# Second attention layer: h in 20 pieces with two own PSUM banks, rectified scores in SBUF

## The reference

```python
h = (x @ W).reshape(N, heads, out_ch)          # N = 1024; x has 1024 values, heads * out_ch = 512
a_src = jnp.einsum('nhc,hc->nh', h, att_src)
a_dst = jnp.einsum('nhc,hc->nh', h, att_dst)
e = jax.nn.leaky_relu(a_src[src] + a_dst[dst], 0.2)
m = jax.ops.segment_max(e, dst, num_segments=N)
ex = jnp.exp(e - m[dst])
s = jax.ops.segment_sum(ex, dst, num_segments=N)
out = jax.ops.segment_sum(h[src] * (ex / (s[dst] + 1e-16))[:, :, None], dst, num_segments=N)
```

## Time and profile before

| | us |
|---|---|
| median of 3 runs | 1220.42 |
| span of the profiled execution | 1220.4 |
| second attention layer, first sum of GpSimd to last `counted` | 906.59 to 1123.65 |
| busy over the span: PE, DVE, ACT, POOL | 1052.0, 778.0, 524.2, 625.3 |

### The profile page before, as it was taken

One profiled execution on the slowest core, in us unless ns is written; L12 is line 12 of the kernel. 1 busy time (PEld: TensorE's weight loads), 2 busy tenths in 40 slices (PEclk: granted clock), 3 DMA queues, 4 the chain that ended last, 5 costly groups with the idle time before them and its releaser, 6 DMA issues. The chain is left out here.

```text
span 1220.4 us, 17917 instructions
## 1 busy us (share of the span) xinstructions
PE 1052.0 (86%) x5617; PEld 744.6 (61%) x5622; DVE 778.0 (64%) x1724; ACT 524.2 (43%) x752; POOL 625.3 (51%) x503
## 2 busy tenths in 40 slices
PE   3999899989599999999298799888898888777897
PEld 1454577778477777777055488787773434433575
DVE  6988578628233333332495889996368777787855
ACT  2234544231111111111133478889537776766323
POOL 1000458302557555543410587999478777685242
PEclk9999899855599999999589799999989999989899
DMA  3000003044388999992510111211012111172551
GB/s 117 1 0 1 1 1 137 2 170 151 132 285 296 301 302 307 303 306 94 182 35 1 37 45 43 87 53 36 9 39 69 36 53 35 37 242 72 179 173 42
DMA packets 107987, 134.57 MB, mean 110 GB/s; under 512 B 30240, under 2 KB 76040, under 8 KB 107792
## 3 DMA queue, kind: packets, MB, share of 16 engines
q1 hardware_dynamic: 92720, 112.68, 28.4%
q0 software_dynamic: 15200, 21.04, 5.3%
HBM read 135.03 MB, written 27.45 MB: 133 GB/s over the span
## 5 line engine op out<-in xcount | busy, mean ns | idle before, releaser
L2347 POOL TENSOR_TENSOR am<-CT,qb 128x1024 f32<-128x1024 f32 x128 | 302.2, 2385 | 29.5 <-ACT PT L2376 17.4
L2369 ACT ACTIVATE PS<-adb,ab 128x1024 f32<-128x1024 f32 x128 | 143.1, 1118 | 89.4 <-DVE am L2474 88.2
L2474 DVE TENSOR_TENSOR am<-PS,am 128x1024 f32<-128x1024 f32 x128 | 156.4, 1222 | 37.3 <-ACT PS L2369 30.2
L2468 DVE CUSTOM_DVE_ANT_0 masked<-PS,mask 128x1024 f32<-128x1024 f32 x128 | 156.2, 1220 | 32.4 <-issue 30.6
L2580 PE MATMUL PS<-PT,h 128*65 128x512 f32 x256 | 122.8, 611 | 36.6 <-ACT PT L2376 25.1
L1232 DVE COPY yo<-PS 128x512 f32<-128x512 f32 x64 | 44.3, 691 | 168.5 <-PE PS L1170 163.1
L2567 PE MATMUL PS<-h,PT 128*128 128x129 f32 x1024 | 128.0, 283 | 22.0 <-ACT PT L2376 12.2
L2376 ACT ACTIVATE PT<-am,as 128x1024 f32<-128x1024 f32 x128 | 145.2, 1134 | 0.3 <-DVE am L2474 0.3
L2567 PEld LDWEIGHTS PS<-h,PT 128*128 128x128 f32 x1024 | 121.1, 196 | 30.5 <-issue 18.2
L1197 ACT ACTIVATE hT<-PS,b1T 128x128 f32<-128x128 f32 x128 | 40.0, 363 | 214.8 <-PE PS L1162 195.7
L1162 PE MATMUL PS<-xgT,w1r 128*128 128x128 f32 x1024 | 125.8, 276 | 0.0
(11 more groups left out here) (426 smaller groups left out, 1777.9 us busy)
## 6 DMA issues: line engine op xcount, KB each, us to landing
w2r<-in_L_ffn_W SPq DMA_DIRECT2D x64, 512.0 KB
w1r<-in_L_ffn_W SPq DMA_DIRECT2D x64, 512.0 KB
adb<-a_scratch SPq DMA_DIRECT2D x16, 512.0 KB, 4.0
qb<-q_scratch SPq DMA_DIRECT2D x14, 512.0 KB, 3.8
wc<-in_L_gnn_W SPq DMA_DIRECT2D x4, 1024.0 KB, 9.2
w1x<-in_L_ffn_W SPq DMA_DIRECT2D x2, 2048.0 KB, 11.0
w2x<-in_L_ffn_W SPq DMA_DIRECT2D x2, 2048.0 KB, 9.3
w1x<-in_L_ffn_W SPq DMA_DIRECT2D x7, 512.0 KB, 5.4
```

Source lines behind the costliest of these rows:

```text
L2347: pool.tensor_tensor(am[:, k % RING, :], CT[:, s, :], qb[:, hd % 2, :], ALU.add).then_inc(s_sum, 1)
L2369: act.activation(RELU, adb[:, hd % 2, :], ACT.Relu, bias=ab[:, s, hd:hd + 1]).then_inc(s_relu, 1)
L2468: dve.tensor_tensor_reduce(masked[:], wide(row_bank(hd)), mask[:, t, :], 1.0, -3.0e38, ALU.subtract, ALU.max, mrow[:, hd % 2, t:t + 1]).th ...
L2474: dve.tensor_tensor(am[:, k % RING, :], RELU, am[:, k % RING, :], ALU.add).then_inc(s_all, 1)
```

## The change

The rectified scores of the second layer go to a new tile `rl` in SBUF instead of banks 4 and 5. These two banks go to the pieces of h that are made between the pairs, in turn. Those pieces are 20 of one tile by 128 columns instead of ten of twice that, behind 20 pairs; a piece waits only for the copy of the piece two before it, and `rows` waits for no piece. Copies come two pairs behind instead of three. The first attention layer stays as it was.

```diff
+        rl = place("rl", [P, N], F32, 102 * KIB)
...
-            RELU = wide(4)
+            RELU = rl[:] if final else wide(4)
...
             def unit_bank(i):
-                return i % 2 if final else (0, 3, 0)[i]
+                if final:
+                    return i % 2 if i < H0 else 4 + i % 2
+                return (0, 3, 0)[i] if i < H0 else 3
...
-                UNITS = [[(t, 0, slice(0, FH), slice(0, FH))] for t in range(NT)] + quarters
-                H0 = 6
-                H_AT = (0, 1), (0, 3), (1, 1), (1, 5), (2, 1), (2, 5), (3, 5), (4, 1), (4, 5), (5, 1)
+                UNITS = [[(t, 0, slice(0, FH), slice(0, FH))] for t in range(UP_FRONT)]
+                for half, tiles in ((0, range(UP_FRONT, NT)), (1, range(NT))):
+                    UNITS += [[(t, half, slice(q * FQ, (q + 1) * FQ), slice(0, FQ))] for q in range(2) for t in tiles]
+                H0 = UP_FRONT
+                FIRST_HALF = UP_FRONT + 2 * (NT - UP_FRONT)
+                H_AT = ((0, 1), (0, 2), (0, 3), (0, 4),
+                        (1, 1), (1, 4), (1, 6), (2, 1), (2, 4), (2, 6), (3, 0), (3, 3),
+                        (3, 5), (3, 7), (4, 1), (4, 4), (4, 6), (5, 1), (5, 4), (5, 6))
...
-            LATE = 3 if final else 2
+            LATE = 2
...
-                            sp.wait_ge(s_h, NT)
+                            sp.wait_ge(s_h, FIRST_HALF)
...
-                    def rows(hd, moved):
+                    def rows(hd):
                         pe.wait_ge(s_oT, 2 * hd + 2)
                         wait(pe, s_ev, hd)
-
-                        wait(pe, s_hm, moved)
...
                         if (hd, s) in H_AFTER:
-                            wait(pe, s_hm, H_AFTER[hd, s])
                             if final:
-                                if H_AFTER[hd, s] == NT:
+
+                                wait(pe, s_hm, max(H0, H_AFTER[hd, s] - 1))
+                                if H_AFTER[hd, s] == FIRST_HALF:
                                     pe.wait_ge(s_w2[1], 16)
-                                wait(pe, s_ev, hd if s > 2 else hd - 1)
                             else:
+                                wait(pe, s_hm, H_AFTER[hd, s])
                                 wait(pe, s_xm, turns)
-                            h_tile(H_AFTER[hd, s], 3)
+                            h_tile(H_AFTER[hd, s], unit_bank(H_AFTER[hd, s]))
```

More of the change, by code:

```diff
@@ L2198, in attend @@
                         for q in range(2) for t in range(0, NT, 2)]
+            UP_FRONT = 6
             if final:
-                UNITS = [[(t, 0, slice(0, FH), slice(0, FH))] for t in range(NT)] + quarters
-                H0 = 6
-                H_AT = (0, 1), (0, 3), (1, 1), (1, 5), (2, 1), (2, 5), (3, 5), (4, 1), (4, 5), (5, 1)
+                UNITS = [[(t, 0, slice(0, FH), slice(0, FH))] for t in range(UP_FRONT)]
[6 more added lines that the diff above has]
+                        (3, 5), (3, 7), (4, 1), (4, 4), (4, 6), (5, 1), (5, 4), (5, 6))
             else:
@@ L2219, in h_units @@
                 if hd < HEADS // 2:
-                    return s + 1
-                return NT + (hd - HEADS // 2) // 2 * (NT // 2) + s // 2 + 1
+                    return s + 1 if s < UP_FRONT else UP_FRONT + hd // 2 * (NT - UP_FRONT) + s - UP_FRONT + 1
+                return FIRST_HALF + (hd - HEADS // 2) // 2 * NT + s + 1
             FIRST = {**{s: ((2, s),) for s in range(5)}, 5: ((2, 5), (2, 6)), 6: ((2, 7),), 7: ((3, 0),)}
@@ L2421, in _ @@
                     act.wait_ge(s_q0, 1)
-                    act.copy(qb[:, 0, :], RELU).then_inc(s_q0m, 1)
+                    act.copy(qb[:, 0, :], wide(4)).then_inc(s_q0m, 1)
                     if not final:
@@ L2426, in _ @@
                     act.wait_ge(s_q0m, 1)
+                    if final:
+                        act.wait_ge(s_as, 2)
                     relu(0)
@@ L2437, in _ @@
                         if (hd, s) in H_MOVED:
-                            h_moved(H_MOVED[hd, s], 3)
+                            h_moved(H_MOVED[hd, s], unit_bank(H_MOVED[hd, s]))
                         if final and s == 0 and hd:
@@ L2645, in _ @@
                         if (hd, s) in H_AFTER:
-                            wait(pe, s_hm, H_AFTER[hd, s])
                             if final:
-                                if H_AFTER[hd, s] == NT:
+                                wait(pe, s_hm, max(H0, H_AFTER[hd, s] - 1))
+                                if H_AFTER[hd, s] == FIRST_HALF:
                                     pe.wait_ge(s_w2[1], 16)
-                                wait(pe, s_ev, hd if s > 2 else hd - 1)
                             else:
+                                wait(pe, s_hm, H_AFTER[hd, s])
                                 wait(pe, s_xm, turns)
-                            h_tile(H_AFTER[hd, s], 3)
+                            h_tile(H_AFTER[hd, s], unit_bank(H_AFTER[hd, s]))
                         if final and s == 2 and hd:
-                            rows(hd - 1, h_before(hd, s))
+                            rows(hd - 1)
                         if final:
@@ L2663, in _ @@
                     if final:
-                        rows(HEADS - 1, len(UNITS))
+                        rows(HEADS - 1)
                         tail.pe_end(pe)
```

## The result

On the same chip the changed kernel took 1250.51 us (median of 4 runs, 1249.65 to 1251.89) against 1221.28 before: a ratio of 1.024 [1.0223, 1.0258]. Slower was forecast, by 19.8 us; it is 29.8 between the two profiled executions (1250.2 against 1220.4), inside the range, and half as much again as the sum.

The account below looks back on a forecast made before the run. The prediction took a ring of mutual waits through TensorE, about 6 us a head, to bound the second layer; 3.9 + 8.6 + 7.3 = 19.8 us on 1220.4 gave 1240.2 us, with an 8 in 10 range of 1223 to 1258.

Parts of the forecast that it names:

- The root: VectorE's counted, with both operands in SBUF, and GpSimd's sum take turns; counted's mean 2 us or more instead of 1.22.
- five heads: Stretch from q(2) to q(7) in the second layer: 28.14 us a head, 140.7 against 132.07, so +8.6 us.
- The turn of 3.31 us a pair: Second layer, where VectorE and GpSimd both have work: 2.22 + 1.09 us a pair instead of 2.48.
- The relu, taken at nothing: ScalarE's rectified tile going to SBUF: 0 to 0.015 us each, at most 1.0 us over 64 pairs, taken as 0.
- the much slower rival: q's small operations stand behind counted, two a head, 15 us; TensorE's lower clock some 4 us: 1259 us, chance 0.12.
- The first paragraph: What bounds the kernel before: mutual waits through TensorE in the second layer, 26.4 us a head, about 6 us of it waits.
- the even rival: Turns are taken but VectorE and GpSimd always have a next one ready, so idle vanishes: 1223.8 us, chance 0.10.
- start to q(2): Second layer's start until GpSimd's row work for head 2: from 933.95 to 937.9, so +3.9 us.
- the end: Heads 6 and 7, from q(7) to the end of the last counted: 64.9 us against 57.63, so +7.3.
- the idle at q: At each head's q neither engine holds the interface for some time: 1.5 us idle, 0.14 more for a fresh sum.
- q itself 1.41: Length of GpSimd's row work q, part of a 3.72 us gap between sums in which VectorE does two counted (2.2).
- the idle of 1.5 us and seven times 0.6: Heads 6 and 7: 1.5 us at q(7), and 0.6 in each of some seven pairs with GpSimd on full buffers.

Follow-up runs that it names:

- run with fills: Changed kernel with each GpSimd sum of the second layer replaced by three constant fills, edges and row q left out: 1211.89 us in one run.
- one maximum a pair: Changed kernel leaving out one of eight masked maxima of each head from head 2 on (tile 5, a constant instead): 1242.36 us, ratio 1.0169.
- no pair overfull: Changed kernel with q's five operations on VectorE and the masked maxima of tiles 5 and 7 left out from head 2 on: 1245.03 us, ratio 1.0202.

## Why the prediction was right, and where its sum was short

The root was right. `counted` had a mean of 2.0 us, up to 3.37; in the five heads VectorE no longer waits for the turned sums, and of its 2.28 us waits before a maximum one is left (2.23, at 941.97); the scores alone bring the loss and the pieces alone a gain. GpSimd's sum, expected near 3.1 us, has 2.98. The turn of 3.31 us a pair, taken from one collision in the earlier trace rows, is what the steady pairs take (3.30). The relu, taken at nothing, rose from 1.119 to 1.151 and lies in ScalarE's idle time, as was said, though its upper bound of 0.015 us was too low. The range held because its upper end was set by the much slower rival, not because the sum was near.

The first paragraph took the kernel before for more even than it was. Its 26.4 us a head are the mean of four heads of 27.03 to 27.05 and one of 23.91, between these two starts of q in GpSimd's timeline of before:

```profile
988.04 0.21 POOL L2309 TENSOR_TENSOR zx<-mrow,ab 128x8 f32<-128x8 f32 x1 [5.69 <-DVE mrow L2468]
...
1011.95 0.21 POOL L2309 TENSOR_TENSOR zx<-mrow,ab 128x8 f32<-128x8 f32 x1 [2.54 <-DVE mrow L2468]
```

It is the one head of the five that has no piece of h ahead of `rows` (`H_AT` has no (3, 1)), and in it VectorE does not stand 3.35 us for the turned sums; head 5 has a single piece too, but ahead of `rows`, and takes 27.04. So the trace of before bore out the reading of the earlier trace rows, and showed what such a piece cost: 3.1 us a head, in four heads 12.5 us, near the 14 that the pieces alone gave. The nearness of 26.4 to 26.5, on which the even rival leaned, was one of a mean over unlike heads.

The Trainium skill (SBUF — State Buffer, "Who interferes with whom") adds that a GpSimd instruction that only writes SBUF does not contend in this way. The run with fills agrees (1.224 us).

By terms, predicted and measured: the first sum 0 and +1.07; start to q(2) +3.9 and +3.4; five heads +8.6 and +13.55; the end +7.3 and +11.55; behind it 0 and +0.2. Together 29.8. The first sum is no cost of the change that the runs show: in the experiments it starts anywhere from 905.0 to 908.8 us.

**The step that failed in the heads is the idle at q**, "q itself 1.41" and the 1.5 us idle that follow from it. q's TENSOR_SCALAR reads SBUF and stands behind a `counted`: 1.11 us instead of 0.26, so q takes 2.27. The much slower rival named this mechanism and priced it twice a head; it comes once, q stays below the 2.5 us that were to decide for that rival, and a head costs 0.85 more. (Its other half, a lower clock in the end, came, 0.85 against 0.91, but the runs show no price for it.) The stop of GpSimd at q is 2.31 + 2.27 = 4.58 us from 996.84 on (4.83 in the head shown above), VectorE fits two `counted` into it, and 4.58 - 2 x 1.09 + 0.14 = 2.54 are lost beyond the turns of 8 x 3.31 = 26.48: 29.02, measured 29.07. The same sum with each kernel's own stop gives 26.48 + 2.36 - 1.09 + 0.14 = 27.89 with one maximum a pair (measured 27.71 to 27.87), and 26.48 + 3.38 - 1.09 + 0.14 = 28.91 with q on VectorE (28.93). With no pair overfull, stop 3.92 and two `counted`, it gives 28.36 for 28.63, so there 0.27 is not explained. Sums in halves, where a pair takes 3.45 and the stop is 2.36 with one `counted`, come to 27.60 + 2.36 - 1.09 + 0.14 = 29.01 (measured 28.85 to 29.14). By this sum a head is bound by the turns and by the part of GpSimd's stop that VectorE does not fill, whatever the stop is for: the maximum and q in the changed kernel, full buffers with q on VectorE. It was found after the runs, with the stops and the `counted` in them read from each trace, and no run was forecast by it.

**At the end the mis-sized term is the idle of 1.5 us and seven times 0.6.** With turns of 59.2 us that made 64.9; the stretch took 69.18, so with the turns as priced the idle is 10.0 and not 5.7 us. The timeline of both engines in heads 6 and 7 of the changed kernel:

```profile
1086.34 14.46 POOL L2358 TENSOR_TENSOR am<-CT,qb 128x1024 f32<-128x1024 f32 x5
...
1089.69 2.85 DVE L1923 TENSOR_TENSOR x_res<-x_res,a_zo 128x512 f32<-128x512 f32 x1
1092.47 3.36 DVE L2487 TENSOR_TENSOR am<-rl,am 128x1024 f32<-128x1024 f32 x1
1095.76 2.84 DVE L1923 TENSOR_TENSOR x_res<-x_res,a_zo 128x512 f32<-128x512 f32 x1
1098.52 3.36 DVE L2487 TENSOR_TENSOR am<-rl,am 128x1024 f32<-128x1024 f32 x1
...
1104.18 5.19 POOL L2358 TENSOR_TENSOR am<-CT,qb 128x1024 f32<-128x1024 f32 x2 [3.38 <-ACT PT L2387]
```

VectorE asks twice a pair, each time just behind the start of a sum, and waits the sum out twice: 1098.52 - 1092.47 = 6.05 us for one pair, in which GpSimd does two sums. It gets ahead, fills its buffers and stands 3.38 us, and so again later (4.08, 3.73 and 3.60), besides 4.00 for qb. I had put such stops at 0.6 net of what VectorE does in them; how much VectorE fills of each was not worked out. VectorE is busy, much of it waiting, for 66.63 of 69.18 us, and the scores in PSUM there gave 9.1 us back. That `counted` is the cause in the end is so shown; how its cost splits into turns and stops is not.

## What to carry to other kernels

Before an operand moves from PSUM to SBUF, look at what GpSimd reads beside it: here 1.22 us became 2.0 to 3.4, inside a busy instruction, where neither engine's idle column shows it. Price such a pair by its turns, then add each stop of the one engine less what the other fits into it; and ask of every small operation near a long one what it stands behind, since its own length says nothing. A change of two halves is tried by halves: here small pieces were worth 14 us and the scores in SBUF cost more than twice as much.

## What the runs showed of the hardware that was not expected

- VectorE's TENSOR_SCALAR with a single SBUF operand, zy<-zx on 128 x 8, also waited out a sum: 2.32 us instead of 0.17. The Trainium skill (SBUF — State Buffer, "Who interferes with whom") lists tensor_scalar among the operations that can enter a mode in which they contend; this row agrees.
- Turns go by whole instructions: halving the sums took 1.0 us off the longest `counted` (3.37 to 2.35), and beside fills that only write `counted` took no turn (1.224 us).
- A small operation waits as long as a large one: 0.17 us on 128 x 8 became 2.13 and 2.19 behind a sum, and GpSimd's 0.21 became 1.20 behind a `counted`.
- ScalarE's relu of 128 x 1024 into SBUF takes 1.151 us, into PSUM 1.119, while its exp into SBUF takes 1.135.
